# Who scales and adds the last query tile's turned states beside an attention: ScalarE and GpSimd in place of VectorE

## What is computed

```
x  = x + tanh(g_xattn) * ssm(ctx, layernorm(x))      # per sample, 512 channels e, 512 time steps t, 16 states n
   dA    = exp(delta[e,t] * A[e,n])                  # decay
   state = state * dA + delta[e,t] * u[e,t] * B[n,t] # scan over t
   y     = sum_n state[e,n,t] * C[n,t] + D[e] * u    # what the change touches: the sum over n
   y     = y * silu(z)
x  = x + tanh(g_ffn) * decoder_layer(layernorm(x))   # attention with rotary embedding, then the experts
```

## Time and profile before

| | us |
|---|---|
| median of 3 runs | 1853.08 (1849.81 to 1853.17) |
| profiled execution: its own time | 1852.96 |
| profiled execution: its span | 1851.2 |
| busy PE / DVE / ACT / POOL | 1504.1 / 1180.0 / 892.6 / 806.3 |
| mean granted clock of PE | 0.878 |

### The profile page before, as it was taken

One profiled execution on the slowest core, in us unless ns is written; L12 is line 12 of the kernel. 1 busy time (PEld: TensorE's weight loads), 2 busy tenths in 40 slices (PEclk: granted clock), 3 DMA queues, 4 the chain that ended last, 5 costly groups with the idle time before them and its releaser, 6 DMA issues.

```text
span 1851.2 us, 26612 instructions
## 1 busy us (share of the span) xinstructions
PE 1504.1 (81%) x9104; PEld 1157.0 (63%) x9104; DVE 1180.0 (64%) x1731; ACT 892.6 (48%) x1974; POOL 806.3 (44%) x809
## 2 busy tenths in 40 slices
PE   5246787777967778877869798979999999999994
PEld 2134454555645555545547566768787899999973
DVE  4689758997579986599964443343333566665545
ACT  3443246775356763567742565111122666666510
POOL 0587026663156541366533221124332455555544
PEclk8555896988967898978889899989999999999997
DMA  5620001111101211002103210932220777777464
GB/s 184 260 76 29 1 24 29 59 57 34 42 18 39 72 41 33 9 29 58 47 28 113 100 36 24 352 103 80 80 86 1 285 248 268 236 258 248 168 215 162
DMA packets 94485, 195.74 MB, mean 106 GB/s; under 512 B 8768, under 2 KB 25664, under 8 KB 91024
## 3 DMA queue, kind: packets, MB, share of 16 engines
q1 hardware_dynamic: 89232, 177.26, 28.0%
q0 software_dynamic: 5120, 16.78, 2.7%
HBM read 140.40 MB, written 53.61 MB: 105 GB/s over the span
## 4 chain that ended last, share of the span: by engine, by line
PE 41%; issue 6%; DVE 6%; POOL 3%; ACT 2%; DMA 0%; DVEq 0%; SPq 0%; ACTq 0%; POOLq 0%
PE scores L588 20%; PE bank L588 11%; PE bank L770 2%; POOL yab L2279 2%; PE bank L720 2%; DVE YA L1626 1%; PE bank L652 1%; DVE HS L1616 1%; PE scores L707 1%; PE bank L735 1%; PE bank L997 1%; POOL lal L2272 1%; ACT bank L1174 0%; DVE nm L1668 0%; PE scores L710 0%
## 5 line engine op out<-in xcount | busy, mean ns | idle before, releaser
L2095 POOL TENSOR_TENSOR GB<-DU,BB 128x512 f32<-128x512 f32 x256 | 325.7, 1293 | 70.0 <-DVE DL L1598 46.0
L652 PE MATMUL bank<-ident,HS 128*128 128x128 f32 x896 | 183.0, 339 | 171.8 <-DVE YA L1626 115.7
L1616 DVE TENSOR_TENSOR_SCAN HS<-bank,GB 128x512 f32<-128x512 f32 x224 | 272.9, 1218 | 41.2 <-ACT bank L1174 16.3
L652 PEld LDWEIGHTS bank<-ident,HS 128*128 128x128 f32 x896 | 124.7, 171 | 217.3 <-DVE YA L1626 145.8
L1174 ACT ACTIVATE bank<-DL,aneg 128x512 f32<-128x512 f32 x224 | 154.8, 691 | 133.9 <-DVE HS L1616 133.0
L1626 DVE SCALAR_TENSOR_TENSOR YA<-bank,Ct,YA 128x512 f32<-128x512 f32 x224 | 165.9, 740 | 20.1 <-PE bank L652 18.0
L720 PE MATMUL bank<-ident,EX 128*128 128x128 f32 x640 | 131.4, 306 | 41.5 <-ACT PT L1217 23.4
L588 PE MATMUL scores<-xth,wgh 128*128 128x256 f32 x552 | 158.0, 286 | 2.1 <-DVE fa L1977 1.2
L588 PE MATMUL scores<-xth,wgl 128*128 128x256 f32 x552 | 156.1, 283 | 0.0
L588 PE MATMUL scores<-xtl,wgh 128*128 128x256 f32 x552 | 156.0, 283 | 0.0
L1209 ACT ACTIVATE EX<-scores,nm 128x128 f32<-128x128 f32 (+3 forms) x256 | 132.1, 520 | 33.0 <-DVE nm L1668 31.9
(11 more groups left out here) (272 smaller groups left out, 3731.4 us busy)
## 6 DMA issues: line engine op xcount, KB each, us to landing
wgr<-wffn_in SPq DMA_DIRECT2D x108, 384.0 KB, 6.5
wdr<-wffn_in SPq DMA_DIRECT2D x81, 256.0 KB, 2.9
BB<-b_scratch SPq DMA_DIRECT2D x64, 256.0 KB, 3.2
xg<-V SPq DMA_DIRECT2D x1, 11776.0 KB, 40.4
xr<-xg SPq DMA_DIRECT2D x23, 512.0 KB, 5.8
yg<-ysb SPq DMA_DIRECT2D x23, 512.0 KB, 6.5
hah<-hhd SPq DMA_DIRECT2D x5, 1024.0 KB, 13.4
hal<-hhd SPq DMA_DIRECT2D x5, 1024.0 KB, 15.1
```

Of the source, the lines that this page charges most:

```text
L652: mm = nc.tensor.transpose(state_bank(s, q)[:, et * P:(et + 1) * P], HS[:, n % 2, et, tt * P:(tt + 1) * P], ident[:])
L1616: nc.vector.tensor_tensor_scan(HS[:, n % 2, et, :], decay_bank(s, k), GB[:, k % 4, :], 0.0, ALU.mult, ALU.add).then_inc(scan_done, 1)
L2095: nc.gpsimd.tensor_tensor(GB[:, k % 4, :], DU[:, et, :], BB[:, n % 2, :], ALU.mult).then_inc(gb_ready, 1)
```

## The change

Beside an attention (s > 0) the last query tile of every state, block q' = 4n + 3, no longer goes through `add_state`. ACT scales the turned bank by Ct into a new SBUF buffer SC (`scale_state`), and POOL adds SC to YA[3] (`add_scaled`). `scale_state` stands in ACT's list ahead of `decay k+4`; `add_scaled` stands in POOL's list between `driven k+1` and `driven k+2`, one unit later. The call `add k-1` is taken out of DVE's list and nothing else there moves. PE's next `turn_states`, and `turn_z`, wait for the new semaphore `scaled` where they waited for that tile's add; the last product of `scan_out` waits for POOL's. SC lies on the place of `xd`, which is idle at that time, so `xdbl` waits for POOL. To make room for the two semaphores, the count of `ddiag_s` goes into `consts`, and `xs_ld` and `h2_ld` become one semaphore, so that the first add of the experts' part on DVE (line 1959) waits for the loads of h2r too.

```diff
@@ -101,6 +101,9 @@
         YA = mid("YA", [P, T4, L])
+        so = ExitStack()
+        SC = arena(so)("SC", [P, L])
+        so.close()
         xd = mid("xd", [N3, L])
@@ -258,7 +261,8 @@
         x2_st = [sem(f"x2_stored{i}") for i in range(T4)]
-        consts, rows_made, ddiag_s = sem("consts"), sem("rows_of_constants_made"), sem("ddiag_made")
+        consts, rows_made = sem("consts"), sem("rows_of_constants_made")
+        scaled, y_pl = sem("states_scaled"), sem("y_added_by_pool")
         z_bn, z_mv, z_norm, z_n, z_t, z_done = [sem("z_" + n) for n in
@@ -292,7 +296,7 @@
         hh_ld = [sem(f"h2_parts_loaded{b}") for b in range(B)]
-        xs_ld, h2_ld = sem("x2_loaded"), sem("h2_rows_loaded")
+        xs_ld = sem("x2_and_h2_rows_loaded")
         wg_in = [[sem(f"gate_up_loaded{r}_{c}") for c in range(KC)] for r in range(2)]
@@ -383,6 +387,15 @@
             return PB
+        def by_pool(s, q):
+            return s > 0 and q % T4 == T4 - 1
+        def adds(s, q):
+            before = sum(not by_pool(r, p) for r in range(s) for p in range(NB))
+            return before + sum(not by_pool(s, p) for p in range(q))
@@ -518,7 +531,7 @@
                     sp.dma_start(h2r[:, T4 * b:T4 * b + T4, :], h2d[T4 * b:T4 * b + T4].rearrange("t p h -> p t h")
-                                 ).then_inc(h2_ld, 16)
+                                 ).then_inc(xs_ld, 16)
@@ -614,7 +627,7 @@
                 if tt == 0:
-                    pe.wait_ge(ddiag_s, T4)
+                    pe.wait_ge(consts, 7 + T4)
                     pe.wait_ge(cv_tap, 12 * s + 12)
@@ -646,8 +659,11 @@
                     pe.wait_ge(scan_done, NB * s + T4 * n + T4)
-                if q > (s == 0):
-                    at(pe, y_acc, NB * s + q - (s == 0))
+                last = q - (2 if s == 0 else 1)
+                if last >= 0 and by_pool(s, last):
+                    pe.wait_ge(scaled, NS * (s - 1) + n)
+                elif last >= 0:
+                    pe.wait_ge(y_acc, adds(s, last + 1))
                 for et in range(T4):
@@ -656,7 +672,8 @@
                 if tt < 2:
-                    pe.wait_ge(y_acc, NB * s + NB)
+                    pe.wait_ge(y_acc, adds(s, NB))
+                    at(pe, scaled, NS * s)
                 else:
@@ -1121,6 +1138,7 @@
                 at(act, b_stored, 16 * s)
+                at(act, y_pl, NS * (s - 1))
                 nc.scalar.activation(xd[:], HT[0][0:N3, :], ACT.Copy, scale=0.5).then_inc(xd_ready, 1)
@@ -1173,6 +1191,14 @@
                                      ).then_inc(dA_ready, 1)
+            def scale_state(s, n):
+                q = T4 * n + T4 - 1
+                act.wait_ge(hT_ready, NB * s + q + 1)
+                if n == 0:
+                    act.wait_ge(b_stored, 16 * (s + 1))
+                at(act, y_pl, NS * (s - 1) + n)
+                nc.scalar.activation(SC[:], state_bank(s, q), ACT.Copy, scale=Ct[:, T4 - 1, n:n + 1]).then_inc(scaled, 1)
@@ -1288,6 +1314,8 @@
                         finish(b, row, m + 1)
+                    if q > 0:
+                        scale_state(s, q - 1)
                     if 0 < q + 1 < NQ:
@@ -1621,14 +1649,17 @@
                 else:
-                    dve.wait_ge(y_acc, NB * s + q - T4 + 1)
+                    dve.wait_ge(y_acc, adds(s, q - T4 + 1))
                 dve.wait_ge(hT_ready, NB * s + q + 1)
                 for tt in range(T4):
-                    dve.wait_ge(y_acc, NB * s + NB - T4 + tt + 1)
+                    if by_pool(s, tt):
+                        dve.wait_ge(y_pl, NS * s)
+                    else:
+                        dve.wait_ge(y_acc, adds(s, NB - T4 + tt + 1))
                     dve.wait_ge(zT_ready, T4 * s + tt + 1)
@@ -1746,8 +1777,6 @@
                         scan(s, k + 3)
-                    if last:
-                        add_state(s, k - 1)
                     if next_:
@@ -1953,7 +1982,7 @@
                         if m == T4 * EARLY:
-                            dve.wait_ge(xs_ld, 16 * B)
+                            dve.wait_ge(xs_ld, 32 * B)
                         if u:
@@ -2052,7 +2081,7 @@
                 nc.vector.tensor_scalar(ddiag[:, et, :], ident[:], chan[:, et, TAPS + 2:TAPS + 3], 0.5,
-                                        ALU.mult, ALU.mult).then_inc(ddiag_s, 1)
+                                        ALU.mult, ALU.mult).then_inc(consts, 1)
             for r in range(-1, B):
@@ -2093,6 +2122,14 @@
                 nc.gpsimd.tensor_tensor(GB[:, k % 4, :], DU[:, et, :], BB[:, n % 2, :], ALU.mult).then_inc(gb_ready, 1)
+            def add_scaled(s, n):
+                pool.wait_ge(scaled, NS * (s - 1) + n + 1)
+                if n == 0:
+                    pool.wait_ge(yi_done, T4 * s + T4)
+                else:
+                    pool.wait_ge(y_pl, NS * (s - 1) + n)
+                nc.gpsimd.tensor_tensor(YA[:, T4 - 1, :], YA[:, T4 - 1, :], SC[:], ALU.add).then_inc(y_pl, 1)
@@ -2163,18 +2200,21 @@
             def units(b, s):
-                for q in range(-1, NQ + 1):
+                for q in range(-1, NQ + 2):
                     now = 0 <= q < NQ
                     k = T4 * q
-                    if q > 0:
+                    if 0 < q <= NQ:
                         widen(b, q - 1)
                         driven(s, k + 1)
+                    if q > 1:
+                        add_scaled(s, q - 2)
+                    if now:
                         driven(s, k + 2)
-                    if q > 0:
+                    if 0 < q <= NQ:
                         context(b, q - 1)
@@ -2255,7 +2295,7 @@
                         pool.wait_ge(routed, 1)
-                        pool.wait_ge(h2_ld, 16 * B)
+                        pool.wait_ge(xs_ld, 32 * B)
                     nc.gpsimd.indirect_dma_start(xg, bass.IndirectOffsetOnAxis(ap=slot[:, j, t:t + 1], axis=0),
```

## The result

| | before | after |
|---|---|---|
| median of 15 runs each, us | 1851.24 (1848.51 to 1855.98) | 1856.3 (1853.75 to 1860.36) |
| ratio after / before | | 1.0025, 95% interval 1.0017 to 1.0033 |
| profiled execution: own time / span, us | 1852.96 / 1851.2 | 1859.31 / 1857.1 |
| busy PE / DVE / ACT / POOL, us | 1504.1 / 1180.0 / 892.6 / 806.3 | 1503.7 / 1145.4 / 920.0 / 866.6 |
| mean granted clock of PE | 0.878 | 0.873 |

A forecast was written before the change was run, and what follows sets the result against it. Between scans k+3 and k+4 ACT's decay, not DVE's work, was taken as the bound. Lateness left after absorption 7.4, collisions -1.9 and ends -1.1 sum to +4.4 us: 1857.5 us, range 1854.5 to 1862.

The forecast's parts named there:

- The gap is ACT's, gain 0: Scan k+3 to k+4: ACT's decay fills the 2.08 us with or without DVE's add, so removing it gains 0.
- The scaling: New ACT instruction ahead of decay k+4: 0.67 us long, 0.57 until the decay can start, bounds 0.49 and 0.63.
- The lateness: Decay k+4, and so scan k+4, held up by the scaling: 12.7 us in sum over 42 units.
- The absorbed part: Lateness met by DVE's existing waits for the transposes of tile 4q: 5.3 us, leaving +7.4.
- The collisions: Residual's add L1688 on DVE no longer held up by POOL's driven in nine places: -1.9 us.
- The ends of the stretches: Last units of the three stretches: earlier transposes of tile 60 and earlier turn_z, -0.35 us each, -1.1 in all.
- POOL's add and the semaphores at 0: POOL's 48 adds of 1.26 us fit its waits; merged semaphores delay nothing, h2r's loads landing before the experts' add: 0.
- no scan would wait for GB: Sign that the forecast is right: no scan on DVE waits for GB, POOL's driven being ready in time.
- A: Rival: no measurable change, within 0.2%; scaling costs 0.49 with terms at the low end, or more is absorbed; 1855 us, 36%.
- B: Rival: PE's clock rises, all 42 units get the faster transposes and DVE's 16.9 us of waits go; 1840 us, 7%.
- C: Rival: DVE really is the bound and the work taken from it comes back, -35.6 - 3 us; 1814 us, 2%.
- D: Rival: clearly slower; PE cools and all 42 units are slowest kind, 1869 us, or dear scaling with nothing absorbed, 1867; 12%.

The follow-up runs named there:

- the unused scaling: Kernel before plus one ACT Copy a state, result unread, where the change puts its scaling; adds stay on DVE: 1862.8 us, ratio 1.0046.
- the other query tile: Changed kernel with query tile 1 moved to ACT and POOL instead of the last, scaling behind decay k+6: 1838.77 us, ratio 0.9932 to before.
- the best kernel: Changed kernel with query tile 1 moved instead of the last, and POOL's driven k+2 held until state q-2 is turned: 1831.33 us, ratio 0.9876 to before.

## Why the prediction was right, step by step

- **Forecast.** 1857.5 us was given, 1856.3 was measured beside 1851.24 for before; the ratio 1.0025 is +4.6 us on before's 1853.08 that I had, against +4.4 worked out.
- **The gap is ACT's, gain 0** held: 87.2 with the add and without it (the adds left out), and the unused scaling gives the changed kernel's distances.
- **The scaling** was taken as 0.67 and 0.57 until the decay; it is 0.687 and 0.57 to 0.59.
- **The lateness** was set at 12.7 us and is 15.1. The size of each unit's kind was right; the count was not. I had taken the transposes' end of before for each unit. In 6 of the 42 units it lay at 1.15 or more after the scan's start, in the changed kernel in 15. Unit 5 is one: 1.02 before, 1.24 after, and its transposes are of the slow kind in both (1.12 and 1.11 us). So it is mostly their start that moved; those longer than 0.9 us went only from 20 units to 22. The runs do not show what settles the kind.
- **The absorbed part**, 5.3, is 7.1. The larger lateness is not the reason: the smaller of each unit's measured lateness and its wait of before still gives 5.1. The premise that failed is that PE's own chain stays as it is. In unit 9 scan k+4 to k+5 became 0.52 shorter for a lateness of 0.08, since the last tile's transposes took 0.66 instead of 1.11 there and tile 4q's were over 1.73 after scan k+4, where it was 2.25. Both errors are about 2 us and cancel. That is luck: the terms were known less well than the sum came out.
- **The collisions** went as argued from the order of POOL's queue, all nine to 0.75, -1.9. That they are on the path is shown by the kernel in which POOL is held back; what they cost on average may well be more than one trace's 1.95.
- **The ends of the stretches**, -1.1, did not come: 0.14 was gained on the scaling, and 0.25 at tile 60, which lasted in two of the stretches, but 0.46 was lost on the last transposes, which I had taken as 0.66 there. This step failed. Their full size was misjudged too: with the adds out altogether they gave 7.0 us (1.8, 2.6 and 2.6).
- **POOL's add and the semaphores at 0** held, with a run for each. DVE's waits for ACT ahead of the scan rose by 42 us, as asked; POOL's wait for context fell by 128 rather than 50, as most of it moved ahead of its own new add (96.8). That no scan would wait for GB was wrong as a sign: such waits were there before (4.3 us) and stayed (4.8).
- **Rivals.** A (within 0.2%) is not quite excluded: the intervals of the two measurements begin at 1.0017 and 1.0018. Its mechanism did not show: the scaling costs 0.57 to 0.59, not 0.49. B's change of kind did not come: the units with slow transposes became two more, not fewer. C falls by the adds left out. D (1867 to 1869) asked for all units of the slowest kind; 15 are.
- **What I expected of the experiments and missed:** that the call behind the decay would be nearly free (it hid the question who waits for the bank), and that a second scaling would leave the ends of the stretches as they were (3.9 us more).

## What to carry to other kernels

A busy share of 90% does not make an instruction worth removing: look at the gap in which it lies, and at what else would end that gap if it were empty; here one of DVE's adds was worth 0 and the add two places on was worth 0.58 us a unit in its own gap (24.5 us in the 42, of which the next distance gave back 11.4). An instruction given to another engine costs what stands behind it in that engine's list and whoever waits for the buffer it reads, and moving it past one of these moves the wait to the other. Waits that absorb a delay are used up once: with the first 15.1 us of lateness the next distance fell by 7.1, with 29.8 more only by another 3.1.

## What the runs showed of the hardware

An add on DVE with two operands in SBUF takes 0.75 us alone, and up to 1.88 when instructions of POOL are under way (1.80 at 605.78 above, where POOL's own next one took 1.75 instead of 1.31). How much such collisions cost varies from one trace to the next of nearly the same order: an excess over 0.75 of 1.9 us before, 1.5 with only the semaphores changed, 2.8 with the adds left out, 4.0 with the unused scaling; 6.5 with the other query tile. Four transposes of the same form mostly take 0.66 or 1.1 us, and which it is changes with small shifts of the order: the last ones of the three stretches took 0.66 each before and 1.12 or 1.11 after. The granted clock of the stretches, 0.82 to 0.84 before, was 0.86, 0.83 and 0.87 in the best kernel, and 0.78 to 0.80 in the windows of the kernel with the scaling twice; what its gain owes to that and what to the shorter list of DVE, the runs do not separate.
